# Last stage of a four-layer cross-attention network: two transposes of the narrow layer in one bank and one copy, and two steps moved in the queues of ScalarE and VectorE

## What is computed

```
# layer 2 (wide)
h = layernorm(x) * gamma + beta
Q, K, V = h @ Wq, context @ Wk, context @ Wv        # 16 heads of 64
attn = softmax(Q K^T) * scale
x = x + (attn V) @ Wo + bo
# layer 3 (narrow)
q, k, v = x @ Wq^T, context @ Wk^T, context @ Wv^T  # 16 heads of 8
attn = softmax(q k^T * scale)
x = x + (attn v) @ Wo^T + bo
```

## Time and profile before

| | |
|---|---|
| median of 3 runs | 1638.55 us (1637.86 to 1639.41) |
| the profiled execution, its own time | 1642.71 us |
| its span (first to last instruction) | 1640.8 us |
| mean granted TensorE clock | 0.993 |
| PE busy | 1589.6 us (97%) |
| DVE busy | 1203.8 us (73%) |
| ACT busy | 1046.1 us (64%) |
| POOL busy | 751.0 us (46%) |

### The profile page before, as it was taken

How to read it: one execution, slowest core, us unless ns; L and a number is a source line. 1 busy time by engine, 2 the same in 40 slices (tenths; PEclk the granted TensorE clock), 3 DMA queues, 4 the chain that set the end, 5 groups by cost and what they waited for, 6 DMA issues and landing times. The chain is left out here.

```text
span 1640.8 us, 49726 instructions
## 1 busy us (share of the span) xinstructions
PE 1589.6 (97%) x18236; PEld 1357.4 (83%) x18236; DVE 1203.8 (73%) x2401; ACT 1046.1 (64%) x3075; POOL 751.0 (46%) x1113
## 2 busy tenths in 40 slices
PE   7999999999999999999999999987999999999998
PEld 6788888878888888878988887876888898988987
DVE  5877777777777777766757676557878887888873
ACT  4777777777777777763326665445666665666654
POOL 3444444444444444442314552644555454555640
PEclk9999999999999999999999999999999999999999
DMA  6766776688667766650051000004445446444440
GB/s 189 206 188 183 192 190 184 186 228 221 193 184 192 189 184 189 186 162 1 0 135 30 2 3 2 1 1 142 144 148 170 138 131 184 125 145 143 139 122 10
DMA packets 229002, 220.07 MB, mean 134 GB/s; under 512 B 20610, under 2 KB 225092, under 8 KB 228740
## 3 DMA queue, kind: packets, MB, share of 16 engines
q1 hardware_dynamic: 228836, 217.79, 46.8%
HBM read 116.01 MB, written 101.71 MB: 133 GB/s over the span
## 5 line engine op out<-in xcount | busy, mean ns | idle before, releaser
L972 POOL TENSOR_TENSOR L_probs<-L_probs,L_inv_sum 128x1024 f32<-128x1024 f32 x128 | 242.8, 1897 | 88.3 <-DVE L_inv_sum L860 88.3
L748 ACT ACTIVATE L_probs<-L_scores,L_neg_max 128x128 f32<-128x128 f32 x512 | 182.7, 386 | 136.2 <-DVE L_neg_max L840 136.2
L834 DVE TENSOR_REDUCE L_row_max<-L_scores 128x8 f32<-128x1024 f32 x128 | 156.2, 1220 | 41.6 <-PE L_scores L605 41.6
L866 DVE STREAM_TRANSPOSE L_squares<-L_probs 128x1024 f32<-128x1024 f32 x125 | 152.9, 1223 | 0.7 <-POOL L_probs L972 0.7
L2113 POOL TENSOR_TENSOR L2L_w_probs<-L2L_w_probs,L2L_w_inv_sum 128x1024 f32<-128x1024 f32 x64 | 121.4, 1896 | 60.8 <-DVE L2L_w_inv_sum L1951 59.3
L1810 ACT ACTIVATE L2L_w_probs<-L2L_scores,L2L_w_neg_max 128x128 f32<-128x128 f32 x256 | 91.3, 385 | 72.7 <-DVE L2L_w_neg_max L1931 72.7
L2129 POOL TENSOR_SCALAR L2L_n_k_apart<-L2L_n_qk,quad_mask 128x128 f32<-128x128 f32 x124 | 53.8, 448 | 176.7 <-ACT L2L_n_qk L1799 176.7
L605 PE MATMUL L_scores<-L_kT,L_qT 64*128 64x128 f32 x2048 | 131.8, 278 | 0.9 <-ACT L_kT L737 0.9
L605 PEld LDWEIGHTS L_scores<-L_kT,L_qT 64*128 64x128 f32 x2048 | 119.4, 188 | 12.5 <-ACT L_oT L737 8.1
L656 PEld LDWEIGHTS L_ring<-L_probsT,L_v 128*64 128x64 f32 x2048 | 110.5, 137 | 22.2 <-issue 18.5
L656 PE MATMUL L_ring<-L_probsT,L_v 128*64 128x128 f32 x2048 | 126.6, 276 | 2.2 <-ACT L_oT L737 1.0
(11 more groups left out here) (257 smaller groups left out, 4472.7 us busy)
## 6 DMA issues: line engine op xcount, KB each, us to landing
L_relay<-L_squares SPq DMA_DIRECT2D x125, 512.0 KB, 3.4
L_probsT<-L_relay SPq DMA_DIRECT2D x500, 128.0 KB, 3.5
L2L_relay<-L2L_w_squares SPq DMA_DIRECT2D x62, 512.0 KB, 3.6
L2L_w_probsT<-L2L_relay SPq DMA_DIRECT2D x248, 128.0 KB, 3.0
ctx_blocks<-ctx_turned SPq DMA_DIRECT2D x48, 128.0 KB, 3.7
out_x<-x SPq DMA_DIRECT2D x32, 64.0 KB, 2.8
ctx_turned<-ctxT SPq DMA_DIRECT2D x1, 1536.0 KB, 7.1
L0a_wq<-in_L_xattn_Wq SPq DMA_DIRECT2D x2, 256.0 KB, 3.0
```

The source lines that it names most:

```text
L748: done = nc.scalar.activation(slot_probs(at, 0)[:, n, :], scores[:, 0, r, i, :], ACT.Exp, scale=layer_of(at).scale, bias=neg_max[:, n:n + ...
L834: nc.vector.tensor_reduce(row_max[:, s, :], slot(s), AX.X, ALU.max).then_inc(max_ready[s], 1)
L866: nc.vector.transpose(squares[:, at.n % 2, :, SLOT_HEADS * s:SLOT_HEADS * (s + 1), :] .rearrange("p j h a -> p h j a"), slot_probs(at, s). ...
L972: nc.gpsimd.tensor_tensor(to, to, inv_sum[:, :, s, :].unsqueeze(3) .to_broadcast([TOKENS, 2, GROUP, TOKENS]), ALU.mult).then_inc(divided, 1)
```

## The change

Three edits, all in `wide_and_narrow`.

1. `n.hT` and `n.oT` become one fill, `n.ho`, of one bank: the transpose of x goes to its columns 0 to 127, that of the attention rows to columns 128 to 255. One ACT copy of 256 columns takes both into a new tile `n_hoT`, from which `n_queries_keys` and `n_project_out` read their halves. In turns in which only one of the two exists, the copy has 128 columns. Each turn from 4 to 32 has one fill less, so every later fill of the turn stands one place further forward in the ring.
2. In ACT's queue the copy of `w.q1` stands ahead of the narrow exponential of group 0. Before, it stood between those of groups 0 and 1.
3. In DVE's queue the third search for narrow maxima (group 2) stands ahead of `w_turned_h`, which takes `w.hT` out of its bank. Before, it stood behind it.

```diff
@@ -1354,7 +1354,7 @@
     QUARTERS = range(4)
     order = [("w.PV0", -1, "act"), ("w.PV1", -1, "act"), ("n.PV", -4, "act"), ("w.q0", 2, "act"), ("w.Wo", -1, "dve"),
              ("n.D", -4, "dve"), ("w.kv0", 0, "act"), ("w.kv1", 0, "dve"), ("w.kv2", 0, "act"), ("w.kv3", 0, "act"),
-             ("n.hT", -1, "act"), ("n.oT", -4, "act"), ("w.hT", 3, "dve"), ("w.q1", 2, "act"), ("n.qk", -1, "act"),
+             ("n.ho", 0, "act"), ("w.hT", 3, "dve"), ("w.q1", 2, "act"), ("n.qk", -1, "act"),
              ("n.v", -3, "act"), ("n.Wo", -4, "dve"), ("n.mT", -2, "dve")]
     first, last = 0, BATCHES + 3
     DVE_NORMALISES = 3
@@ -1374,6 +1374,14 @@
     def makes_keys_values(t):
         return real(t) or real(t + 1) if t % 2 else real(t + 2)
 
+    def turns_rows(t):
+        return real(t - 1) or real(t - 4)
+
+    def filled_in(name, t, lag):
+        if name.startswith("w.kv"):
+            return makes_keys_values(t)
+        return turns_rows(t) if name == "n.ho" else real(t + lag)
+
     def keys_made(b):
         return b // 2 * 2 - 2
 
@@ -1382,7 +1390,7 @@
 
     ring = Fills(filled_before + [(name, t + lag, engine) for t in range(first, last + 1)
                                   for name, lag, engine in (turned_by_pe if t == LAST_WIDE + 1 else []) + order
-                                  if (makes_keys_values(t) if name.startswith("w.kv") else 0 <= t + lag < BATCHES)])
+                                  if filled_in(name, t, lag)])
     chunks = INNER // 128
     half_rows = 64
     GROUP = 4
@@ -1421,8 +1429,7 @@
         w_sums = sb("w_sums", [TOKENS, 2, 2, GROUP])
         w_inv_sum = sb("w_inv_sum", [TOKENS, 2, 2, GROUP])
 
-        n_hT = sb("n_hT", [DIM, TOKENS])
-        n_oT = sb("n_oT", [DIM, TOKENS])
+        n_hoT = sb("n_hoT", [DIM, 2, TOKENS])
         n_qk = sb("n_qk", [128, 2, 2, TOKENS])
         n_q_part = sb("n_q_part", [128, 2, 2, TOKENS])
         n_k_apart = sb("n_k_apart", [128, 2, GROUP, TOKENS])
@@ -1696,20 +1703,23 @@
                                                ident[:, :])
                 filled_by(last, "n.D")
 
-            def n_transpose_h(b):
-                await_emptied(pe, "w.Wo", b)
-                filled_by(nc.tensor.transpose(start_fill("n.hT", b)[:, 0:TOKENS], x[:, b, :], ident[:, :]), "n.hT")
-
-            def n_transpose_o(b):
-                hold_clock("n.oT", b, 3)
-                await_emptied(pe, "n.D", b)
-                filled_by(nc.tensor.transpose(start_fill("n.oT", b)[:, 0:TOKENS],
-                                              n_rows_o[:, :, :].rearrange("p h d -> p (h d)"), ident[:, :]), "n.oT")
+            def n_transpose_rows(t):
+                if real(t - 4):
+                    hold_clock("n.ho", t, 3 if t > LAST_WIDE + 1 else 0)
+                to = start_fill("n.ho", t)
+                if real(t - 1):
+                    await_emptied(pe, "w.Wo", t - 1)
+                    last = nc.tensor.transpose(to[:, 0:TOKENS], x[:, t - 1, :], ident[:, :])
+                if real(t - 4):
+                    await_emptied(pe, "n.D", t - 4)
+                    last = nc.tensor.transpose(to[:, TOKENS:2 * TOKENS], n_rows_o[:, :, :].rearrange("p h d -> p (h d)"),
+                                               ident[:, :])
+                filled_by(last, "n.ho")
 
             def n_queries_keys(b):
-                await_emptied(pe, "n.hT", b)
+                await_emptied(pe, "n.ho", b + 1)
                 to = start_fill("n.qk", b)
-                nc.tensor.matmul(to[:, 0:TOKENS], N.wq[:, :], n_hT[:, :], start=True, stop=True)
+                nc.tensor.matmul(to[:, 0:TOKENS], N.wq[:, :], n_hoT[:, 0, :], start=True, stop=True)
                 filled_by(nc.tensor.matmul(to[:, TOKENS:2 * TOKENS], N.wk[0:N.kv_rows, :], ctxT[0:N.kv_rows, b, :],
                                            start=True, stop=True), "n.qk")
 
@@ -1720,8 +1730,8 @@
 
             def n_project_out(b):
                 hold_clock("n.Wo", b, 2 if b == LAST_WIDE else 0)
-                await_emptied(pe, "n.oT", b)
-                filled_by(nc.tensor.matmul(start_fill("n.Wo", b)[:, 0:DIM], n_oT[:, :], N.wo[:, :],
+                await_emptied(pe, "n.ho", b + 4)
+                filled_by(nc.tensor.matmul(start_fill("n.Wo", b)[:, 0:DIM], n_hoT[:, 1, :], N.wo[:, :],
                                            start=True, stop=True), "n.Wo")
 
             w_keys(-2)
@@ -1771,10 +1781,8 @@
                     n_both_scores(t, (2, 3), (0, 1))
                 if t == LAST_WIDE + 3:
                     n_turn_back(t - 4)
-                if real(t - 1):
-                    n_transpose_h(t - 1)
-                if real(t - 4):
-                    n_transpose_o(t - 4)
+                if turns_rows(t):
+                    n_transpose_rows(t)
                 if real(t + 3):
                     w_transpose_h(t + 3)
                 if real(t + 2):
@@ -1880,14 +1888,14 @@
                     n_exponentiate(t - 3, 3)
                 if makes_keys_values(t):
                     w_keys_values(t, (0, 2, 3))
-                if real(t - 1):
-                    copied("n.hT", t - 1, n_hT[:, :], bank("n.hT", t - 1)[:, 0:TOKENS])
-                if real(t - 4):
-                    copied("n.oT", t - 4, n_oT[:, :], bank("n.oT", t - 4)[:, 0:TOKENS])
+                if turns_rows(t):
+                    low, high = (0 if real(t - 1) else 1), (2 if real(t - 4) else 1)
+                    copied("n.ho", t, n_hoT[:, low:high, :].rearrange("p a q -> p (a q)"),
+                           bank("n.ho", t)[:, TOKENS * low:TOKENS * high])
+                if real(t + 2):
+                    w_queries(t + 2, 1)
                 if real(t - 3):
                     n_exponentiate(t - 3, 0)
-                if real(t + 2):
-                    w_queries(t + 2, 1)
                 if real(t - 3):
                     n_exponentiate(t - 3, 1)
                 if real(t - 1):
@@ -2067,10 +2075,11 @@
                     w_turn_squares(t + 1, 0)
                 if makes_keys_values(t):
                     w_keys_values(t, 1)
+                if real(t - 2):
+                    n_find_maxima(t - 2, 2)
                 if real(t + 3):
                     w_turned_h(t + 3)
                 if real(t - 2):
-                    n_find_maxima(t - 2, 2)
                     n_find_maxima(t - 2, 3)
                 if real(t - 4):
                     n_finish(t - 4)
```

## The result

| | before | after |
|---|---|---|
| median | 1638.98 us (4 runs, 1637.86 to 1642.18) | 1630.85 us (4 runs, 1629.52 to 1632.02) |
| profiled execution, its own time | 1642.71 us | 1632.02 us |
| its span | 1640.8 us | 1628.9 us |
| mean granted clock | 0.993 | 0.991 |

The ratio is 0.9944, with a 95% interval of 0.9931 to 0.9957. The medians differ by 8.1 us; the interval allows 7 to 11 us. The forecast was 1632.0 us.

What follows compares the result with a forecast made beforehand. PE bounds the kernel, with ACT's three copies of keys or values ahead of `w.q1` in its chain of waits. 25 x 0.325 = 8.1 us, less 1.3 (relay) and 0.25 (tail), is 6.55: 1638.55 to 1632.0 us, range 1629.0 to 1636.0.

Steps and rivals of the forecast that it cites:

- 0.325 us per turn: Turns 4 to 28: `w.q1` starts at 1404.855 in place of 1405.18, saving 0.325 us in each turn.
- PE itself needs three transposes of 0.165 us: Ahead of `w.q1`: three transposes from 1404.36 at turn 29's pitch end at 1404.855, after the middle copy's 1404.69.
- My bound from above, 0.40: Most that a turn could save: the whole gap ahead of `w.q1`, 0.40 us.
- my own bounds for it, 0.23 to 0.40: Saving per turn: at least 0.23 us if the middle copy releases late, at most 0.40 us.
- The low end of the range: 25 turns at 0.40 us, 10 us, nothing returned to relay or tail: about 1629.0 us.
- Relay, -1.3 us: SP's queue, held by twelve loads: gains of turns 7, 8, 15 and 16 are waited for in turns 9 and 17.
- the first rival: Turn 9: its wait grows to 1.94 us and lowers the clock, losing 1.8 us: 1633.8 us; chance 0.16.
- Tail, -0.25 us: Turns 30 to 32: `n.qk` waits longer for the 256-column copy; 0.25 us lost, bounds 0 and 0.8.
- The moves at 0: ACT's copy of `w.q1` ahead of an exponential costs 0; DVE's earlier maximum gives `n.mT` 0.7 us margin, costed at 0.
- Second: Turn's end: the next wait, at `n.qk` or first scores, uses up the gain: 1635.5 to 1638.8 us; chance 0.13.
- third rival: Late exponentials on ACT hold PE from the turn's start: 0.53 lost for 0.325 saved, 1644.0 us; chance 0.07.
- a cover that I had put at 1.0: Exponentials hold PE only if the last ends more than 1.0 us after the first scores, at their second half.

Runs made afterwards that it cites:

- another order with the same release: Kernel before, no joint bank, `w.q1` ahead of `w.hT` on PE and in the ring, ACT's and DVE's queues made to suit: 1632.90 us, ratio 0.9962.
- the loads spread: Twelve context loads of turns 8 and 16 spread over four turns, three in each: 1621.96 us on the change, 1634.95 us on the kernel before.
- the late exponentials: Whole change, with both narrow exponentials moved behind ACT's copies of `n.qk` and `n.v`: 1638.19 us in a single run.

## Why the prediction was right, and where its sizes were off

**The mechanism.** What the prediction said happens: `w.hT` waits for DVE's copy, `w.q1` for the middle copy on ACT, the copies leave the chain, and all that follows moves along. The joint fill alone does it, the moves alone do not, and another order with the same release does most of it.

**0.325 us per turn: it was 0.50.** The step that was off is "PE itself needs three transposes of 0.165 us", taken from turn 29 as time without a wait. That row has a wait in it. ACT's three copies of that turn, in the kernel before:

```profile
1575.83 1.57 ACT L1799 ACTIVATE L2L_w_v<-L2L_ring 128x512 f32<-128x512 f32 x3 [1.39 <-PE L2L_ring L1616]
```

With 0.49 us from one to the next and 0.60 us for one, the middle copy ends at about 1576.91, 0.05 us ahead of `w.q1`: the distance from a copy's end that the prediction itself read in turn 18. In the changed kernel 0.16 us holds for the first two transposes only. `w.hT` follows after 0.11 us, and `w.q1` after another 0.11, so `w.q1` starts 0.38 us after the first transpose and not 0.495. That makes 0.44 us. The other 0.05 us is in `w.q1` itself: its eight records take 1.11 us for 1.16 now that it no longer starts after a wait, and `n.mT` stands 1.89 us behind its start for 1.94. My bound from above, 0.40, took only the gap ahead of `w.q1` and forgot that the wait ahead of `w.hT` goes as well: 0.26 + 0.40 were to be had, less two pitches of 0.11. That is why the gain lay outside of my own bounds for it, 0.23 to 0.40. (The low end of the range, too, is 1628.55 by its terms and not 1629.0.)

**Relay, -1.3 us: it was -2.6 to -4.9.** The place was right, and the part that I described has nearly the size that I gave it; two things came on top. Set against a normal turn of its kernel, turn 9 was 1.5 us longer before and 5.0 us now, turn 17 4.6 and 5.0 us. So turn 17 waited for 0.4 of the 1.0 us that turns 15 and 16 had gained. In turn 9 the wait grew from 1.29 to 3.03 us, by 1.7. Of that 1.0 is the gain of turns 7 and 8; the rest goes with SP, which took 6.78 us for the twelve loads, where it had been 6.47, and 2.78 us to send the four parts back at 1240 us, where it had been 1.83. The profile does not show why it was slower. The other 1.8 us of turn 9 are the clock: the first rival came true in the profiled execution, to which I had given 0.16.

**Tail, -0.25 us: no loss to be seen.** The wait ahead of `n.qk` in turns 30 to 32 grew from 0.26 to 0.47 us, as worked out, but the tail from the start of turn 30 is 61.20 us for 61.39. The wait for the relay in turn 31 went from 0.90 to 0.23 us. In each trace the clock also falls once in the tail: in the changed kernel just ahead of that wait, in the kernel before later, in turn 32. So what made up for the longer waits cannot be told apart.

**The moves at 0.** Right within what can be told. DVE's move had a use that I did not see, in turns 2 and 3; in the turns for which I gave it a margin it was not needed. ACT's move cost nothing, and gave nothing.

**Second and third rival.** No new wait used the gain up: the turn kept all of it. For the third the late exponentials are the test: ACT did keep to its order, and the exponentials' end does stop PE once it is late enough: for 0.2 us, when it lies 0.95 us behind the first scores. The rule of the Trainium skill ("TensorE: Matmul & The Clock Gate", section "Architectural detail: the array is 16× 32×32, not 1× 128×128") that ScalarE's queue is strictly first in, first out agrees with these rows. The point from which it decides is 0.75 to 0.81 us after the first scores (the estimate above), so the change used up some 0.6 of a cover that I had put at 1.0.

**The sum.** 25 turns at 0.50 are 12.5 us; with the loads spread the traces show 12.7 and the medians 13.0. Less 3.4 to 4.9 at the relay it is 8 to 9. The forecast of 6.55 had 8.1 for the turns, too small by 4.4, and 1.55 for all losses, too small by 1.9 to 3.4. That it came within 1.2 us of the median is in part luck: these two errors cancel.

## What to carry to other kernels

In a ring of banks each fill waits for the one that stands a ring's length ahead: read off which copy that is, and ask whether a fill less, or another order, makes it an earlier one. When a turn gets shorter, look for the queue that does not scale with it, and measure the change again with that queue relieved; here a quarter of the gain by the traces (3.4 of 12.7 us) was lost to twelve loads that were started at once. Two waits in a row on the critical engine are one term: cost what is left when both are gone, and before you take a distance between instructions for PE's own pitch, make sure that no copy ends just ahead of the second one.

## What the runs showed that was not expected

Whether a wait for the relay lowers the clock is not decided by its length in these runs. PE, the weighing behind that wait, first in the kernel with the late exponentials (turn 9), then in the joint fill with ACT's move (turn 9):

```profile
1247.22 1.09 PE L1641 MATMUL L2L_ring<-L2L_w_probsT,L2L_w_v 128*64 128x128 f32 x16 [2.25 <-DMA L2L_w_probsT<-L2L_relay]
```

```profile
1245.14 1.09 PE L1641 MATMUL L2L_ring<-L2L_w_probsT,L2L_w_v 128*64 128x128 f32 x16 [3.03 <-DMA L2L_w_probsT<-L2L_relay]
```

and the windows of these two turns, in the same order:

```profile
1241.55:1260.98 19.43, 17.14 (x239) 15.62 (x238) 13.03 (x25) 10.78 (x33) 8.75 (x13) 0.91 0.57 167
```

```profile
1239.06:1257.47 18.41, 15.35 (x240) 14.11 (x240) 13.04 (x26) 10.66 (x33) 8.75 (x13) 1.00 0.55 166
```

After 2.25 us of waiting the turn was granted 0.91, after 3.03 us the full 2.4 GHz; the turn with the shorter wait took 1.0 us longer. PE's instructions and their order are the same in both, though not all of its waits. One kernel shows the same by itself: in the joint fill alone, turn 9 had a wait of 2.83 us and was granted 0.91, turn 17 one of 2.73 us and was granted 1.00. Over turns 9 and 17 of the eight traces with the loads together, the clock stayed at 1.00 with waits of 1.15, 1.29, 2.73, 3.00 and 3.03 us, and fell with eleven others, of 1.95 to 3.44 us. The shortest of these, 1.95 us in turn 9 of the kernel with `w.q1` first, is the wait that the first rival asked about. A term for the clock behind such a wait should be put down as a chance, not as a step at some length; and a turn 9 or 17 of one trace need not be that of the other executions in the median.
